# The last layer's experts in two lists of two batches, with the last attention chain and the shared expert between their blocks

## The reference, cut to what matters

```
x = x + tanh(g_xattn[3]) * L3_xattn(ctx, ctx, layernorm(x), ...)    # one head, 32 keys
x = x + tanh(g_ffn[3]) * L3_ffn(layernorm(x), ...)

def L3_ffn(x, router_w, expert_bias, shared_w1, shared_w2, shared_w3, routed_w1, routed_w2, routed_w3):
    # H = 512 hidden in the shared expert, RH = 128 in each of E = 16 routed ones, K = 2
    shared_out = (silu(x @ shared_w1) * (x @ shared_w2)) @ shared_w3
    scores = sigmoid(x @ router_w)
    _, top_idx = top_k(scores + expert_bias, K)
    gates = sum over the two chosen of one_hot(top_idx, E) * scores
    routed_out = sum over e of (silu(x @ w1[e]) * (x @ w2[e])) @ w3[e] * gates[:, e]
    return shared_out + routed_out
```

## Time and profile before

| what | us |
|---|---|
| median of 3 runs (lowest, highest) | 933.48 (932.61, 933.59) |
| the profiled execution: time, span | 939.1, 937.3 |
| TensorE busy | 780.0 (83%) |
| VectorE busy | 562.6 (60%) |
| GpSimd busy | 391.1 (42%) |
| ScalarE busy | 372.7 (40%) |
| mean granted TensorE clock | 0.929 |

### The profile page before, as it was taken

The page is one execution under the profiler, slowest core; times in us unless marked ns, Lnnn a source line. Parts: engine busy times, 40 slices in busy tenths (PEclk is TensorE's granted clock), DMA queues, the critical chain, the costliest instruction groups (busy, mean ns, idle before and its releaser), DMA issues.

```text
span 937.3 us, 14236 instructions
## 1 busy us (share of the span) xinstructions
PE 780.0 (83%) x3968; PEld 557.1 (59%) x3968; DVE 562.6 (60%) x1820; ACT 372.7 (40%) x832; POOL 391.1 (42%) x381
## 2 busy tenths in 40 slices
PE   2789978998989968677689798799989887988884
PEld 1367765666666635455568788465645553645552
DVE  3345667888889647664333276897876644534454
ACT  0033424353535434432335434446555655223331
POOL 3000003454546524346354343556446673335661
PEclk9999988999999978885789899899999999898998
DMA  5011399950000031000657753100140000022314
GB/s 130 1 34 45 97 333 332 333 174 0 1 1 1 1 95 29 17 18 33 197 166 196 216 158 90 46 1 1 34 135 13 13 12 13 18 59 71 83 47 135
DMA packets 83923, 79.18 MB, mean 84 GB/s; under 512 B 23548, under 2 KB 72918, under 8 KB 83720
## 3 DMA queue, kind: packets, MB, share of 16 engines
q1 hardware_dynamic: 76208, 69.43, 25.8%
q0 software_dynamic: 5024, 8.54, 2.7%
q10 hardware_dynamic: 2616, 0.30, 0.2%
HBM read 40.28 MB, written 39.85 MB: 85 GB/s over the span
## 4 chain that ended last, share of the span: by engine, by line
PE 54%; DVE 22%; issue 10%; ACT 5%; POOL 4%; DMA 2%; another core or an unknown queue 2%; SPq 1%; DVEq 0%; POOLq 0%; ACTq 0%
PE psum L1164 48%; DVE hb L2312 2%; DVE hb L2313 1%; POOL s L735 1%; DVE hb L2310 1%; DVE mr L1977 1%; PE psum L1235 1%; PE psum L1625 1%; ACT hb L967 1%; DMA l_hi<-y 1%; PE psum L1363 1%; DVE x L1950 1%; PE psum L1695 1%; DVE l_lo L1893 1%
## 5 line engine op out<-in xcount | busy, mean ns | idle before, releaser
L672 POOL TENSOR_TENSOR h_lo<-hb,h_hi 128x512 fp32r<-128x512 f32 x68 | 87.8, 1294 | 122.8 <-ACT h_hi L900 122.7
L1164 PE MATMUL psum<-xt_hi,wa_hi 128*128 128x512 f32 x272 | 127.7, 469 | 13.3 <-DVE hb L2313 8.6
L740 POOL DMA_INDIRECT y<-xn x93 | 92.4, 993 | 96.4 <-issue 38.1
L882 ACT ACTIVATE hb<-psum 128x512 f32<-128x512 f32 x136 | 81.0, 596 | 81.5 <-PE psum L1164 81.3
L1164 PE MATMUL psum<-xt_lo,wa_hi 128*128 128x512 f32 x272 | 107.7, 396 | 0.0
L667 POOL TENSOR_TENSOR hb<-hb,wsb 128x512 f32<-128x512 f32 x64 | 82.7, 1292 | 53.3 <-DVE hb L2310 47.9
L1164 PEld LDWEIGHTS psum<-xt_hi,wa_hi 128*128 128x128 f32 x272 | 52.3, 192 | 36.0 <-DVE hb L2313 14.2
L1164 PE MATMUL psum<-hb,wa_hi 128*128 128x512 f32 x136 | 70.0, 595 | 0.5 <-POOLq L669 0.5
L1164 PE MATMUL psum<-l_lo,l_hi 128*128 (+1 forms) x204 | 60.2, 394 | 12.1 <-issue 7.3
L643 POOL TENSOR_TENSOR rstd<-veps,neghalf 128x4 f32<-128x4 f32 x20 | 20.3, 1017 | 118.6 <-DVE veps L1871 117.9
L2310 DVE TENSOR_TENSOR hb<-hb,psum 128x512 f32<-128x512 f32 x68 | 46.0, 684 | 37.8 <-ACT hb L882 27.8
(11 more groups left out here) (371 smaller groups left out, 1747.1 us busy)
## 6 DMA issues: line engine op xcount, KB each, us to landing
s<-l_lo SPq DMA_DIRECT2D x20, 1386.0 KB, 16.3
l_hi<-in_pack SPq DMA_DIRECT2D x24, 322.0 KB
l_lo<-in_pack SPq DMA_DIRECT2D x22, 322.0 KB
xn<-s SPq DMA_DIRECT2D x93, 66.0 KB
y_in<-y SPq DMA_DIRECT2D x8, 256.0 KB, 3.9
l_hi<-y SPq DMA_DIRECT2D x8, 256.0 KB, 5.9
stage<-in_L_ffn_W SPq DMA_DIRECT2D x12, 128.0 KB, 2.4
y<-xn POOLq DMA_INDIRECT x93
```

The lines of the kernel that those rows point to most:

```text
L672: pool.tensor_tensor(h_lo[:, k % 3, :], hb[:, k % 4, :], h_hi[:, k % 3, :].bitcast(F32), ALU.subtract).then_inc(q["hlo_pool"], 1)
L740: pool.indirect_dma_start(y3, bass.IndirectOffsetOnAxis(xe3[:, j % XE, 128:129].bitcast(I32), 0), xe3[:, j % XE, 0:128], None, bounds_chec ...
L882: act.activation(hb[:, k % 4, :], G[k % 2][:, :], ACT.Silu).then_inc(q["sg_done"], 1)
L1164: return pe.matmul(o, l, r, start=start, stop=stop, skip_group_check=True)
```

## The change

The fourth layer's experts get two lists, one for batches 0 and 1 and one for batches 2 and 3, each with its own part of `s3` and 31 blocks, 62 together. The first list's counts and table move into the third layer's feed-forward (places 55 to 64), and its blocks are the first thing in stage 7. What was the first part of stage 7 now stands in the passes of the loop: batch 3's chain and the end of batch 2's at passes 0 to 24 (`CH_TAIL`; `chain` is called at the end of each pass on every engine), the shared expert in halves of 256 columns at passes 2, 3, 5, 6, ... 47, 48 (`SH_UP`), its down products in quarters at passes 14 to 17, 26 to 29, 38 to 41 and 50 to 53 (`SH_DOWN`). To find banks for this, the block loop's transposed rows, transposed hidden rows and down results have one bank each instead of two (only the up and gate product keeps two), and the shared expert has one bank, `G[0]`, for both of its products. The read back, combine and store of batches 0 and 1 are issued inside the loop. In the second layer's attention, TensorE transposes step i's probabilities ahead of step i + 3's scores, ScalarE copies them ahead of the exp of step i + 3, and `STEP1` moves the router's steps and gives the copy of the transposed rows a step of its own (`rows`).

```diff
-CAP3 = B * S
-NB3 = 2 * B * S // 128 + E3 - 1
+CAP3 = HALF * S
+NP3 = 2 * HALF * S // 128 + E3 - 1
+NB3 = 2 * NP3
+REG3 = 128 * 146
...
-STEP1 = dict(mom=(5, 9, 14, 16), scl=(5, 9, 14, 17), xt=(6, 10, 15, 18), logits=(7, 11, 16, 19), shift=(7, 11, 16, 19),
+STEP1 = dict(mom=(5, 9, 13, 16), scl=(6, 10, 14, 17), xt=(6, 10, 14, 18), rows=(7, 11, 15, 18), logits=(7, 11, 15, 19),
...
+CH_TAIL = dict(mom6=0, scl6=2, xt6=3, scores=4, exp=5, norm=6, pt=7, ptc=7, val=8, up=8, scl7=10, xt7=11, logits=12, top=13,
+               choose=14, cum=15, slots=15, scatter=16)
+CH_LATER = {(2, "slots"): 71, (2, "scatter"): 72, **{(3, k): SH_AT + v for k, v in CH_TAIL.items()}}
...
-SH_UP = {SH_AT + t: i for i, t in enumerate((0, 1, 2, 5, 9, 10, 14, 15, 18, 19, 20, 21))}
-SH_DOWN = {SH_AT + t: n for n, t in enumerate((11, 17, 22))}
-COUNT_PE = [SH_AT + t for t in (17, 18, 19)]
+SH_UP = {2 + 3 * i // 2: i for i in range(8 * B)}
+SH_DOWN = {14 + 12 * n + k: (n, k) for n in range(B) for k in range(TB)}
+COUNT3 = [(55, 58, 61), (SH_AT + 15, SH_AT + 16, SH_AT + 17)]
+TABLE3 = [(56, 60, 64), (SH_AT + 15, SH_AT + 16, SH_AT + 17)]
+ROWS_IN = NP3 + XE + 3
+COMBINE = {NB3 - 6: 0, NB3 - 3: 1}
...
         def gu_out(j):
-            return G[j % 2][:, 0:256]
+            return (G[1], U[0])[j % 2][:, 0:256]
+
+        def xet_out():
+            return W[0][:, 0:128]
+
+        def ht_out():
+            return U[1][:, 0:128]
+
+        def dn_out():
+            return T[:, 0:128]
...
-            sp.wait_ge(q["tabi_done"], 3)
-            sp.wait_ge(d_scat, 16 * 8 * (HALF + B))
             for i in range(NB3):
                 j = NB1 + i
+                part, p = divmod(i, NP3)
+                if p == 0:
+                    sp.wait_ge(q["tabi_done"], part + 3)
+                    sp.wait_ge(d_scat1[part], 16 * 8 * 2 * HALF)
+                if i == ROWS_IN:
+                    rows_in(0)
+                    rows_in(1)
...
+            store(0)
+            store(1)
             for i in range(XE):
                 sp.wait_ge(d_ye[i], 16 * len(range(i, NB1 + NB3, XE)))
...
+            rows_in(2)
+            rows_in(3)
+            store(2)
+            store(3)
...
-                    for g in range(SH_AT, CH_END):
-                        chain(g)
-                    for j in range(NB1, NB1 + NB3):
-                        rows_back(j)
+                    for i in range(NB3 + 5):
+                        chain(SH_AT + i)
+                        if 0 <= i - 5 < NB3:
+                            rows_back(NB1 + i - 5)
...
-                n, c = divmod(i, 4)
+                n, c, h = i // 8, i // 2 % 4, i % 2
                 if i == 0:
                     pe.wait_ge(d_wl, 16 * 7)
...
+                if i >= 1:
+                    pe.wait_ge(q["sh3_done"], i)
+                if i % 8 == 0:
+                    pe.wait_ge(q["c_free"], t2_rows[n])
+                rows = x3t[n][:, 256 * h:256 * h + 256]
+                mm(G[0][:, 0:256], sw1[:, c, :], rows, True, True)
+                mm(G[0][:, 256:512], sw2[:, c, :], rows, True, True).then_inc(q["su3_ps"], 1)
...
-                pe.wait_ge(q["xet_sb"], J - 1)
-                pe.transpose(W[j % 2][:, 0:128], xe3[:, J % XE, 0:128], ident).then_inc(q["xet_ps"], 1)
+                pe.wait_ge(q["xet_sb"], J)
+                pe.transpose(xet_out(), xe3[:, J % XE, 0:128], ident).then_inc(q["xet_ps"], 1)
...
-                if j >= 2:
-                    pe.wait_ge(q["ht3_sb"], j - 1)
-                pe.transpose(U[j % 2][:, 0:128], h3[:, j % 2, :], ident).then_inc(q["ht3_ps"], 1)
+                if j >= 1:
+                    pe.wait_ge(q["ht3_sb"], j)
+                pe.transpose(ht_out(), h3[:, j % 2, :], ident).then_inc(q["ht3_ps"], 1)
...
-                if j >= 2:
-                    pe.wait_ge(q["ye3_done"], NB1 + j - 1)
+                if j >= 1:
+                    pe.wait_ge(q["ye3_done"], NB1 + j)
...
                         if 0 <= i - 4 < NB3:
                             expert_down(i - 4)
-                    for i in range(4 * (B - 1), 4 * B):
-                        shared_up(i)
-                    shared_down(B - 1)
+                        chain(SH_AT + i)
+                        if i in SH_UP:
+                            shared_up(SH_UP[i])
+                        if i in SH_DOWN:
+                            shared_down(*SH_DOWN[i])
...
-                        for n in range(B):
-                            if i == STEP1["logits"][n]:
-                                logits1(n)
+                        probs_t1(i)
                         if i + 3 < 16:
                             scores1(i + 3)
-                        probs_t1(i)
...
                         if 0 <= i - 4 < NB3:
                             expert_out(i - 4)
-                    for i in range(4 * (B - 1), 4 * B):
-                        shared_mult(i)
-                    for b in range(B):
-                        if b == 2:
-                            shared_add(B - 1)
-                        combine(b)
+                        chain(SH_AT + i)
+                        if i - 1 in SH_UP:
+                            shared_mult(SH_UP[i - 1])
+                        if SH_DOWN.get(i - 1, (0, 0))[1] == TB - 1:
+                            shared_add(SH_DOWN[i - 1][0])
+                        if i in COMBINE:
+                            combine(COMBINE[i])
+                    combine(2)
+                    combine(3)
```

197 lines of the change are left out of this document (88 added, 109 removed).

## The result

The changed kernel takes 989.32 us (median of 4 runs, 985.05 to 995.49). The kernel before, run beside it on the same chip, took 933.05 us (4 runs). The ratio is 1.0607, 95% interval 1.0548 to 1.0665: 56 us slower, where +32 was forecast (965, range 936 to 994). The profiled execution took 989.8 us, its span is 988.0.

The account below looks back on a forecast made before the run. In the chain that ended last TensorE held 54% and VectorE 22%. Stage 7 +35.0, second layer's attention -4, third layer's feed-forward +1: +32.0 us, 971.1 on the profile's scale, 965 on the median's; range 936 to 994.

Parts of the forecast that it names:

- passes 2 to 25 without the chain: Stage 7's loop: 2.25 us a pass with shared halves, plus down products and additions, without the last chain; 57.6 us.
- the last chain among the blocks: Stage 7's loop: the last attention and routing chain, run inside the passes, adds 15 us, between bounds 6 and 28.
- passes 50 to 61: Stage 7's passes after the shared halves: 1.46 us a pass allowed, 1.48 counted, plus down pieces and additions; 20.5 us.
- tail: End of stage 7, last result to the end: 17.0 us against 22.0, since only batches 2 and 3 are read back.
- The start behind GpSimd's square root: Start of stage 7: batch 1's last scatter stays behind the square root at 786.84; first block transposed at 791.5.
- The wait behind VectorE's order: Stage 7's loop: shared halves wait for VectorE's expert work; TensorE stands 1.4 us, three passes cost 6.74 us.
- Rival 1: Stage 7: TensorE stays the bound, shared work falls into the sequencer's gaps; 914 us; chance of faster 0.12 in all.
- Rival 2, the low clock: Stage 7's loop: clock at 0.50 throughout the three-pass groups, 1008 us, or in the chain's alone, 987; over 988: chance 0.10.
- the attention of the second layer: Second layer's attention: the new order of steps shortens TensorE's waits; -4 us, out of 10.1 at most.
- The three waits named: Second layer's attention: three TensorE waits of 4.4, 2.9 and 2.8 us, 10.1 in sum, the most that can be won.
- A loss of up to 3: Second layer's attention: scores now stand behind probabilities that GpSimd delivers, costing up to 3 us (16 steps of 0.2).
- the third layer's +1: Third layer's feed-forward: the first half's table adds eleven small products and ten VectorE operations; 1 us, between 0 and 3.

## Why the prediction was right in kind and too small

The sign and the mechanism of the loop held; the size did not. That 989 lies inside the range is in part luck: it is above the forecast's own 948 to 988, in a part of the range that was left open for the low clock, and other errors brought it there. Stage 7 by the prediction's own terms, in us. The 4 us of additions and combines are shared out by their durations, and "without the chain" is measured in the kernel with the chain ahead:

```
term                              forecast   measured
to the first block                   9.1        9.1
passes 0 and 1                       3.0        2.5
passes 2 to 25 without the chain    57.6       61.75
the last chain among the blocks     15         25.9
passes 26 to 49                     61.3       60.2
passes 50 to 61                     20.5       19.6
drain                                6.4        7.6
tail                                17.0       13.6
stage 7                            189.9      200.2
```

**Right.** The start behind GpSimd's square root, to 0.1 us. The wait behind VectorE's order: 6.74 forecast, 6.73 to 6.91 measured, and it goes away with either of its two causes, the order or the single bank. Rival 1, the shared work in the gaps, does not happen in this kernel, but was near to what lies behind the wait: with two banks trios take 5.2 us, three bare passes 5.0.

The Trainium skill (TensorE: Matmul & The Clock Gate, "A second HAM failure mode: psum-queue depth-cycling") tells of a bf16 kernel of 512 columns in which the clock oscillates, since TensorE idles briefly between groups while banks are cycled. The trace does not agree in the trios: the granted clock was 0.98 in passes 26 to 49 of this kernel and 1.00 in its second profile.

**Mis-sized: "the last chain among the blocks".** 15 was put between bounds of 6 and 28, "nearer to VectorE's 13, which can hide least". It is 24 to 26, near the upper bound. The assumption that most of it lies in the chain of waits already counted failed: putting the shared product ahead of it won back only 3 to 5 us in these passes, and without any shared work the cost is about the same. The bounds were sums of busy times, and left out the round trips between engines: alone, the chain keeps TensorE busy for 12.9 of 35.2 us, and VectorE for 15.35. What the runs show instead is that the loop takes up some 9 of these 35 us; the rest comes as TensorE's busy time (13 us, part of it at the lower clock) and as its idle time (13 us, the wait of 6.66 behind ScalarE's stop of 5.37 among it). How much of the idle time is round trips and how much is stops is not shown apart. Rival 2, the low clock, came in part, in the chain's passes: 0.85 between the levels 1.00 and 0.50 is three tenths of the stretch at the lower one, and by the prediction's 2.7 us a trio that makes 6 to 7 of its 22 us, an estimate. It did not come in the trios after them.

**Wrong: "the attention of the second layer", -4.** It is +4.6 (1.4 to 7.8). The three waits named did fall. "A loss of up to 3" for probabilities that GpSimd delivers was 5 to 6.6, and the later first rows (2.4 to 5.2) were not in the sum.

**Smaller ones.** "Passes 2 to 25 without the chain" took 4 us more than forecast: the first two trios behind the start took 10.4 and 7.4 us, at clocks of 0.66 and 0.83, with a stop of 2.34 us. In the passes after 50 the prediction subtracts 0.54 from 1.96 and writes 1.46, where 1.42 comes out; it then counts 1.48. The average of the loop before was 1.59, its undisturbed passes took 1.54, and single banks add 0.12 to 0.18. Passes 50 to 61 came out right all the same, so the additions and combines in them cost less than counted. The tail was 3.4 us shorter than forecast: the reads were issued 3.2 us after the last result (977.63 against 974.43), not 7.15. GpSimd's last scatter started 1.0 us behind the end of the last result; before, it was 4.3 (919.58 against 915.27).

Stage and attention make 45.3 + 4.6 = 49.9 of the 56 (51 to 62 by the interval). The rest, with the third layer's +1 in it, is not resolved. The stage itself varies between executions: 198.1 and 200.2 in the changed kernel, and 154.0 and 152.2 against 154.9 in the two kernels that change only the attention. Kernels with the changed attention reached stage 7 at times from 779.9 to 787.8.

**Open.** What stops ScalarE for 2 to 7 us with no releaser on the core. In passes 2 to 25 these stops sum to 8.0 and 7.6 us in the two profiles of the changed kernel, to 16 to 22 in six other kernels with chain and blocks mixed, 11.8 in the one with two banks, and 2.3 and 2.6 in the two with the chain ahead. The loop of the kernel before, without chain or shared work, had 3.7 too (2.44 and 1.23, ahead of 856.69 and 858.20, next to the stretch of the earlier trace rows). So mixing makes more of them but is not their only source, and what they wait for is not shown. Nor is it shown what one costs: the kernel with the shared work ahead of the chain had 12.5 us more of them and shorter passes.
